# Experts placed among the shared expert's units in a mixture-of-experts layer, with sums that start from zero and are added by accumulating loads

## What is computed

```python
full_logits = x @ gate_w.T                       # 4096 tokens x (8 experts + 1 shared)
rw   = weights of up to 4 experts of each token  # sparse mixer, top-p 0.75, normalised
mask = (rw > 0) & (running count within the expert <= cap)   # cap = 640 tokens an expert
gw   = softmax(full_logits where allowed)
gd   = rw * sum(gw[:, :8])
out  = sum over experts e of gd[:, e] * down_e(silu(gate_e(x)) * up_e(x))   # 128 hidden units
out += gw[:, 8] * shared_down(silu(shared_gate(x)) * shared_up(x))          # 512 hidden units
x    = layernorm(x + out)
```

## Time and profile before

| | |
|---|---|
| median of 3 runs | 3832.75 us (3824.94 to 3836.05) |
| the profiled execution | 3839.45 us, span 3837.9 us |
| mean granted TensorE clock | 0.812 of full speed |
| the changed layer in the span | about 1584 to 1999.5 us |

### The profile page before, as it was taken

One profiled execution on the slowest core, in us unless ns is written; L12 is line 12 of the kernel. 1 busy time (PEld: TensorE's weight loads), 2 busy tenths in 40 slices (PEclk: granted clock), 3 DMA queues, 4 the chain that ended last, 5 costly groups with the idle time before them and its releaser, 6 DMA issues. The chain is left out here.

```text
span 3837.9 us, 34481 instructions
## 1 busy us (share of the span) xinstructions
PE 2848.2 (74%) x12664; PEld 1781.3 (46%) x12664; DVE 1739.6 (45%) x3573; ACT 1272.9 (33%) x1706; POOL 432.6 (11%) x405
## 2 busy tenths in 40 slices
PE   4667677585888888699816666666668888887887
PEld 2645445263333333454514444444446666664554
DVE  4535353543655666164225555555544445431222
ACT  3122131311554555322222222222246666561111
POOL 0110101010000000001541111111110111000000
PEclk9586777767899999799967777777788989997998
DMA  2000000003333332201350000000010100000000
GB/s 57 1 22 0 22 0 0 22 0 110 56 60 68 59 58 40 81 6 48 69 130 11 11 11 11 11 11 11 31 55 12 33 23 23 17 10 18 22 22 33
DMA packets 121228, 123.26 MB, mean 32 GB/s; under 512 B 38160, under 2 KB 108064, under 8 KB 121120
## 3 DMA queue, kind: packets, MB, share of 16 engines
q1 hardware_dynamic: 113440, 111.36, 11.2%
q0 software_dynamic: 7680, 10.49, 1.7%
HBM read 61.11 MB, written 35.26 MB: 25 GB/s over the span
## 5 line engine op out<-in xcount | busy, mean ns | idle before, releaser
L894 DVE TENSOR_REDUCE xattn_tops<-region 128x2 f32<-128x1024 f32 x256 | 305.7, 1220 | 144.4 <-PE region L700 144.3
L832 ACT ACTIVATE xattn_probs<-region 128x1024 f32<-128x1024 f32 x256 | 256.1, 1022 | 154.5 <-PE region L689 153.7
L1923 PE MATMUL region<-psi_fT 128*128 128x512 f32 x512 | 244.8, 622 | 21.9 <-DVE psi_low L2157 21.2
L122 PE MATMUL region<-gla_xT,weights_even 128*128 128x512 f32 (+1 forms) x416 | 197.9, 632 | 0.0
L689 PE MATMUL region<-xattn_qs,xattn_ks 49*128 49x512 f32 x512 | 125.5, 492 | 85.6 <-DVE xattn_tops L894 54.7
L114 PE MATMUL region<-ident,gla_xn 128*128 128x128 f32 x192 | 47.2, 427 | 186.9 <-DVE gla_xn L178 167.1
L114 PE MATMUL region<-ident,mamba_normed 128*128 128x128 f32 x64 | 15.7, 428 | 210.3 <-DVE mamba_normed L176 210.3
L1923 PEld LDWEIGHTS region<-psi_fT 128*128 128x128 f32 x512 | 97.2, 200 | 124.9 <-issue 100.5
L1944 PE MATMUL region<-psi_ctxv,psi_pT 128*128 128x65 f32 x1024 | 138.8, 301 | 20.3 <-issue 19.4
L1944 PEld LDWEIGHTS region<-psi_ctxv,psi_pT 128*128 128x128 f32 x1024 | 137.8, 219 | 29.3 <-issue 29.2
L122 PE MATMUL region<-mamba_xT,weights_odd 128*128 128x512 f32 x320 | 150.4, 632 | 0.0
(11 more groups left out here) (473 smaller groups left out, 5809.5 us busy)
## 6 DMA issues: line engine op xcount, KB each, us to landing
xattn_qs<-xattn_qhi SPq DMA_DIRECT2D x128, 64.0 KB, 2.3
xattn_ks<-xattn_khi SPq DMA_DIRECT2D x128, 64.0 KB, 2.3
gla_x<-in_x SPq DMA_DIRECT2D x8, 512.0 KB, 4.0
x_after_gla<-gla_x SPq DMA_DIRECT2D x8, 512.0 KB, 2.9
xattn_ctxT<-in_ctxT SPq DMA_DIRECT2D x8, 512.0 KB, 3.9
xattn_x<-x_after_gla SPq DMA_DIRECT2D x8, 512.0 KB, 4.1
xattn_qs<-xattn_qlo SPq DMA_DIRECT2D x64, 64.0 KB, 2.4
xattn_ks<-xattn_klo SPq DMA_DIRECT2D x64, 64.0 KB, 2.3
```

The source lines that it names most:

```text
L122: last = st.nc.tensor.matmul(o[0:m, i, :], w[:, c, col + i * P:col + i * P + m], rhs[:, c, :], start=c == 0, stop=c == kc - 1)
L832: A_(probs[:, p % 3, a, :, :], st.region(f"k{v}")[:], ACT.Exp).then_inc(st.emptying(f"k{v}"), 1)
L894: V.tensor_reduce(tops[:, n % 2, t, a::2], st.region(f"q{u}")[:], AX, ALU.max).then_inc(st.emptying(f"q{u}"), 1)
L1923: last = mm(o[:, a, :], fT[:, h, 0, t * P:t * P + P], fT[:, h, 1 + a, :], start=True, stop=True)
```

## The change

Four things change, all in `moe_layer`.

1. The eight experts are spread among the shared units: `turned` gives the unit in which an expert's `turn_rows` and `hidden` stand (18, 19, 20, 21, 23, 24, 25, 26); `down` and `add` follow in the next unit. All five finds of an expert stand in one unit (15 to 22), with its gather at the end.
2. There are six places for gathered rows: three as before, and three in `xT`, where batches' transposed rows are no longer needed. The places in `xT` wait for `begin` of the batches that lay there.
3. `sums` starts from zero: SP writes zeros to all of it (ten DMAs) behind the loads of the layer's input, and stores no rows of `xs` in it. The preamble's clearing and its wait are gone.
4. `finish b`: POOL issues an accumulating load that adds 512 rows of `sums` to the batch's rows in `xs` on the chip. The eight of them wait until all adds have landed. They take the place of SP's eight plain loads.

In `hidden`, ScalarE now writes into the tile `he` itself, instead of `silu`, so that it does not share a buffer with the shared units.

```diff
-        NX, EG, SP_, XE = B * NT, 4, CAP // P, 3
+        NX, EG, SP_, XE = B * NT, 4, CAP // P, 6
...
-        xe = [st.sb(f"xe{i}", [SP_, D]) for i in range(XE)]
+        xe = [st.sb(f"xe{i}", [SP_, D])[:] for i in range(XE - 3)]
+        used = xT[:].rearrange("p b c n -> p (b c n)")
+        xe += [used[:, i * 1280:i * 1280 + 1280].rearrange("p (k d) -> p k d", k=SP_) for i in range(3)]
...
-                V.memset(ye[0], 0.0).then_inc(st.sem("zeroed"), 1)
+                V.memset(picked[:], 0.0)
...
-                sp.wait_ge(st.sem("zeroed"), 1)
-                sp.dma_start(sums[B * T:, :].rearrange("(k p) d -> p k d", p=P), ye[0]).then_inc(st.sem("cleared"), 16)
                 weights.arrive(sp)
-                sp.wait_ge(st.sem("cleared"), 16)
...
+            turned = {18: 0, 19: 1, 20: 2, 21: 3, 23: 4, 24: 5, 25: 6, 26: 7}
             for u in range(B * SHF):
                 b, f = divmod(u, SHF)
-                finds = found[5 * (u - 16) // 2:5 * (u - 15) // 2] if u >= 16 else []
+                finds = [(u - 15, k) for k in range(SP_)] if 15 <= u < 15 + NE else []
+                if u in turned:
+                    yield "turn_rows", turned[u], 0
                 yield "gate", b, f
-                for n, (e, k) in enumerate(finds):
-                    if n == 1:
-                        yield "up", b, f
+                for e, k in finds[0:2]:
                     yield "find", e, k
-                    if k == SP_ - 1:
-                        yield "gather", e, 0
-                if not finds:
-                    yield "up", b, f
+                yield "up", b, f
+                for e, k in finds[2:4]:
+                    yield "find", e, k
+                if u in turned:
+                    yield "hidden", turned[u], 0
                 if f == 1 and b:
                     yield "shared_down", b - 1, 0
+                if u - 1 in turned:
+                    yield "down", turned[u - 1], 0
+                    yield "add", turned[u - 1], 0
+                for e, k in finds[4:]:
+                    yield "find", e, k
+                    yield "gather", e, 0
...
             yield "shared_down", B - 1, 0
-            yield "turn_rows", 0, 0
+            for b in range(B - 1):
+                yield "finish", b, 0
+            yield "measure", 0, 0
             yield "begin", B - 1, 0
-            for e in range(NE):
-                yield "hidden", e, 0
-                if e + 1 < NE:
-                    yield "turn_rows", e + 1, 0
-                yield "down", e, 0
-                yield "add", e, 0
-            for b in range(B + 1):
+            yield "finish", B - 1, 0
+            for b in range(1, B + 1):
...
-                for b in range(B):
-                    sp.wait_ge(st.sem("begun"), b + 1)
-                    sp.dma_start(sums[b * T:b * T + T, :].rearrange("(t p) d -> p t d", p=P), xs[:, b, :, :]).then_inc(
-                        st.sem("sums_out"), 16)
-                sp.wait_ge(st.sem("sums_out"), 16 * B)
-                sp.wait_ge(st.sem("added"), 16 * SP_ * NE)
-                for b in range(B):
-                    sp.dma_start(xs[:, b, :, :], sums[b * T:b * T + T, :].rearrange("(t p) d -> p t d", p=P)).then_inc(
-                        st.sem(f"x_in{b}"), 16)
+                zeros = picked[:].rearrange("p a n -> p (a n)")
+                for n in range((B * T + CAP) // T + 1):
+                    part = sums[n * T:min(n * T + T, B * T + CAP), :].rearrange("(t p) d -> p t d", p=P)
+                    sp.dma_start(part, times(zeros, part.shape[1])).then_inc(st.sem("zeroed"), 16)
...
+                    elif what == "finish":
+                        pool.wait_ge(st.sem("added"), 16 * SP_ * NE)
+                        pool.wait_ge(st.sem("begun"), b + 1)
+                        G.dma_start(xs[:, b, :, :], sums[b * T:b * T + T, :].rearrange("(t p) d -> p t d", p=P),
+                                    accum_op=ALU.add).then_inc(st.sem(f"finished{b}"), 16)
```

More of the change, by code:

```diff
@@ L986, in moe_layer @@
         source, target = st.sb("source", [NE, SP_], U32), st.sb("target", [NE, SP_], U32)
-        picked, ranks = st.sb("picked", [2, P]), f3(expert[:, 0:2 * P], 2)
+        picked, ranks = st.sb("picked", [2, P]), f3(expert[:, 6400:6400 + 2 * P], 2)
         shift = st.sb("shift", [2, NT])
@@ L1033, in order @@
             yield "logits", B - 1, 0
-            found = [(e, k) for e in range(NE) for k in range(SP_)]
+            turned = {18: 0, 19: 1, 20: 2, 21: 3, 23: 4, 24: 5, 25: 6, 26: 7}
             for u in range(B * SHF):
                 b, f = divmod(u, SHF)
-                finds = found[5 * (u - 16) // 2:5 * (u - 15) // 2] if u >= 16 else []
+                finds = [(u - 15, k) for k in range(SP_)] if 15 <= u < 15 + NE else []
+                if u in turned:
+                    yield "turn_rows", turned[u], 0
                 yield "gate", b, f
-                for n, (e, k) in enumerate(finds):
-                    if n == 1:
-                        yield "up", b, f
+                for e, k in finds[0:2]:
                     yield "find", e, k
-                    if k == SP_ - 1:
-                        yield "gather", e, 0
-                if not finds:
-                    yield "up", b, f
+                yield "up", b, f
[3 more added lines that the diff above has]
+                    yield "hidden", turned[u], 0
                 if f == 1 and b:
                     yield "shared_down", b - 1, 0
+                if u - 1 in turned:
[4 more added lines that the diff above has]
+                    yield "gather", e, 0
                 if u < 8:
@@ L1231, in _ @@
                         act.wait_ge(*st.full(f"xe{b}"))
-                        if b == 0:
-                            act.wait_ge(*st.emptied(f"find{NE - 1}_{SP_ - 1}"))
                         if b >= 2:
@@ L1241, in _ @@
                         act.wait_ge(*st.full(f"gue{b}"))
-                        act.wait_ge(*st.emptied(f"gue{b - 1}" if b else f"gu{B - 1}_{SHF - 2}"))
-                        A_(silu[:, 0, :], st.region(f"gue{b}")[:, 0, :], ACT.Silu).then_inc(st.sem("silu"), 1)
+                        if b >= 2:
+                            act.wait_ge(*st.full(f"ye_end{b - 2}"))
+                        A_(he[b % 2][:, 0:T], st.region(f"gue{b}")[:, 0, :], ACT.Silu).then_inc(st.sem("silu_e"), 1)
                         act.wait_ge(*st.full(f"gue_end{b}"))
-                        act.wait_ge(*st.emptied(f"gue_end{b - 1}" if b else f"gu{B - 1}_{SHF - 1}"))
-                        A_(silu[:, 1, 0:P], st.region(f"gue_end{b}")[:, 0:P], ACT.Silu).then_inc(st.sem("silu"), 1)
+                        A_(he[b % 2][:, T:CAP], st.region(f"gue_end{b}")[:, 0:P], ACT.Silu).then_inc(st.sem("silu_e"), 1)
             @block.vector
@@ L1394, in _ @@
                         n = SP_ * b + i
+                        if n == 0:
+                            dve.wait_ge(st.sem("zeroed"), 16 * 10)
                         dve.wait_ge(st.sem("ranked"), n + 1)
@@ L1408, in _ @@
                     elif what == "hidden":
-                        n = SHF * B + 2 * b
-                        dve.wait_ge(st.sem("silu"), n + 1)
-                        if b >= 2:
-                            dve.wait_ge(*st.full(f"ye_end{b - 2}"))
-                        TT(he[b % 2][:, 0:T], silu[:, 0, :], st.region(f"gue{b}")[:, 1, :], ALU.mult).then_inc(
+                        dve.wait_ge(st.sem("silu_e"), 2 * b + 1)
+                        TT(he[b % 2][:, 0:T], he[b % 2][:, 0:T], st.region(f"gue{b}")[:, 1, :], ALU.mult).then_inc(
                             st.emptying(f"gue{b}"), 1)
-                        dve.wait_ge(st.sem("silu"), n + 2)
-                        TT(he[b % 2][:, T:CAP], silu[:, 1, 0:P], st.region(f"gue_end{b}")[:, P:2 * P], ALU.mult).then_inc(
-                            st.emptying(f"gue_end{b}"), 1)
+                        dve.wait_ge(st.sem("silu_e"), 2 * b + 2)
+                        TT(he[b % 2][:, T:CAP], he[b % 2][:, T:CAP], st.region(f"gue_end{b}")[:, P:2 * P],
+                           ALU.mult).then_inc(st.emptying(f"gue_end{b}"), 1)
                     elif what == "down":
@@ L1450, in gather @@
                         pool.wait_ge(*st.full(f"xe_end{e - XE}"))
+                    elif e >= XE - 3:
+                        pool.wait_ge(st.sem("begun"), e - 1)
                     for k in range(SP_):
@@ L1456, in _ @@
                 for what, b, i in work:
-                    if what == "gather" and b < XE:
+                    if what == "gather":
                         gather(b)
-                    elif what == "turn_rows" and b + XE < NE:
-                        gather(b + XE)
                     elif what == "add":
+                        pool.wait_ge(st.sem("targets"), b + 1)
                         if b == 0:
-                            pool.wait_ge(st.sem("targets"), NE)
-                            pool.wait_ge(st.sem("sums_out"), 16 * B)
```

(1 more changed line is left out.)

7 lines of the change are left out of this document (3 added, 4 removed).

## The result

The changed kernel takes 3776.87 us (median of 4 runs, 3765.88 to 3782.18) against 3830.84 us for the kernel before on the same chip: a ratio of 0.9856, 95% interval 0.9829 to 0.9883. The profiled execution took 3782.18 us.

The account below looks back on a forecast made before the run. TensorE bounds the shared units, then POOL's queue sets the end; the next block at 1950.2 instead of 1999.55 us saves 49.3 us, taken from the 3832.75 us median: 3783.4 us, 8-in-10 range 3765 to 3806.

Parts of the forecast that it names:

- the signs that I had named for being wrong: Adds ending behind TensorE's work, load issues longer than the landings' spacing, or a granted clock falling in the units.
- The front: Layer start: without the clearing's wait ahead of the input loads, TensorE starts 5 us earlier, bounds 3 and 6.6.
- The experts move into TensorE's stage and cost all of it there: Shared units: the experts' 60.6 us of TensorE work cost fully there; the adds land by 1899.7 us, TensorE ends at 1908.1.
- the stall rival: Merged stage: `down` on VectorE waits for late adds and holds up TensorE; 12 us go back, 3795 us; chance 0.10.
- The correction of 3.5 us at units 15 to 17: TensorE: a new wait for `steps` of 1 to 2.5 us plus waits for banks add 3.5 us, bounds 2 and 7.
- my count back: Expert and POOL times reckoned backwards from TensorE's end at 1908.1 us, placing the last add's issue at 1895.9 us.
- The accumulating loads' pace: Layer end: at the adds' 146 ns a packet, the DMA engines take 4.67 us a batch; likeliest case, chance 0.45.
- POOL's issue: Issue cost of one accumulating load on POOL: bounds 1.25 and 7.4 us, 5.2 us at 4.7 ns a descriptor.
- the rival in which it sets the pace: POOL's issue of 5.2 us a load paces the layer's end: 35.4 us less, 3797.4 us; chance 0.27.
- 65.5 us: Rival at the layer's end: loads run at nearly the plain rate, saving 65.5 us, 3767.2 us; chance 0.13.
- The tail behind the eighth norm: Layer end: from the start of the eighth norm to the next block takes 10.4 us, as in the kernel before.

Follow-up runs that it names:

- the front alone: The kernel before with only the spare rows' clearing moved behind the input loads and its preamble wait removed: 3826.36 us, ratio 0.9985.
- the changed kernel again: The changed kernel without any edit, measured once more on another experiment's chip: 3777.20 us, ratio 0.9850 to the kernel before.
- the stores-wait profile: The changed kernel with SP's output stores held until all eight accumulating loads have landed: 3771.94 us, ratio 0.9852 to the kernel before.
- the plain load: The changed kernel with POOL's loads not accumulating, so input and shared expert's part are missing from the output: 3771.86 us, ratio 0.9852 to the kernel before.
- the kernel with vector adds: The changed kernel with SP loading `sums` into `xT` and VectorE adding it, replacing the accumulating loads: 3784.72 us, ratio 0.9890 to the kernel before.
- finds in twos: The changed kernel with at most two finds between other products, the first two behind unit 15's `up`: 3776.09 us, ratio 0.9844 to the kernel before.

## Why the prediction was right

The forecast was 49.3 us less by one likely way, and 54 us (3830.84 - 3776.87) were measured. That the spreading carries the saving was right and is shown. That the number came so close is in part luck, because two terms were off in opposite directions: the last add was issued 7.0 us later than I had it (1902.87 against 1895.9 us), and the tail behind it was 10.9 us shorter (43.4 against 54.3). The next block came at 1946.25 us and not at 1950.2. With the first error alone the saving would have been 42 us, with the second alone 60. One of the signs that I had named for being wrong did appear: the granted clock fell in units 15 to 17.

- **The front**, 5 us with bounds 3 and 6.6: TensorE's first transpose came 5.3 us earlier with the front alone and in the changed kernel, and 3.9 us in the changed kernel again, the least of all profiles. Right, and shown by the front alone.
- **The experts move into TensorE's stage and cost all of it there; POOL's adds end before TensorE.** Right: without the spreading the ratio is 0.9986 and not 0.9856. TensorE was busy 20.00 of 20.00 us in the mixed units, at full clock, and ended at 1914.98 us, 8.0 us behind the last landing (and 6.9 us later than my 1908.1). `down` on VectorE never waited for adds, so the stall rival did not occur.
- **The correction of 3.5 us at units 15 to 17**, bounds 2 and 7. The two waits stood where I had put them, 0.74 and 0.52 us. But the stretch from `steps` to expert 0's rows took 42.0 us in the profile after, where my sum has about 36, and 32.8 to 44.3 us over six profiles with the same order: the same products with nearly the same waits differ by 11.5 us with the clock, more than my bounds of 2 and 7 us allow. Because `steps` itself came 3.1 us earlier than I had it (1712.6 us), expert 0's rows were only 2.9 us late. The other 4.1 us of the 7.0 lie between them and the last add: 148.3 us, where my count back has 144.2.
- **The accumulating loads' pace, 4.67 us a batch.** This term was mis-sized: they land 2.65 us apart when nothing else runs. The step that failed is to take the adds' share of engine time, 146 ns a packet, as the pace of the loads. It failed twice. Most of it is that a packet of these loads is not a packet of the adds: by the same division it takes 101 ns, not 146. The rest is that packets overlap on an engine (123.1% in the stores-wait profile), so that 32 of them take 2.65 us, 83 ns each. What I had left out is that the stores share the engines; beside them the last loads land 4.1 to 4.4 us apart. From the first norm's start to the eighth's, 1913.29 to 1935.78 us, it is 3.2 us a load, against 4.67.
- **POOL's issue**, between 1.25 and 7.4 us, estimated at 5.2 us for the rival in which it sets the pace. It is 1.35 us, near the lower bound. If the 0.53 us against the plain load were all for a second read of each row, that would be 1.0 ns a row, not 4.7; the plain load also has a quarter of the packets, so it is at most that. That rival is refuted. The trace agrees with the Trainium skill's statement ("DMA: Bandwidth & Descriptors", "Anatomy of one DMA") that descriptor generation is small. An estimate by its fit for the bytes moved, 1.2 us a batch, does not hold for an accumulating load, which takes 2.65.
- **Where the loads' part ended.** The engines set the pace of the loads, as I had it: the eighth was issued at 1918.28 us, right behind the last `begin`, and landed 17.5 us later behind the others. But their pace alone, 2.65 us, is nearer to the plain rate's 1.53 than to my 4.67. The measured saving lies between the two, 49.3 and 65.5 us.
- **The tail behind the eighth norm**, 10.4 us: 10.5 us.

Two parts of the change bring nothing that these runs can tell: the six places, and the accumulating loads together with the zero start by themselves. What the zero start does is to allow the spreading at all. That follows from the program and not from a run: the adds need no stored rows of `xs`, so that they can begin at unit 19, while before POOL waited ahead of the first add until all eight batches were stored, and so for the eighth batch's `begin`. The accumulating loads are not needed for it, since the kernel with vector adds is spread too.

Open stays why the granted clock stood at half in most of 1716 to 1748 us. It stood there behind a wait of 0.74 us and around one of 0.52 us, and with finds in twos, without these waits, it stayed at full; other differences between the two orders were not tried apart. An earlier fall, around 1704 to 1712 us behind a wait of 2.19 us in the routing, stands with either order. And nearly the same waits went with unlike clocks: in windows of 8 us from 132 us behind the issue on, it was down to 0.50 in three of the six profiles and no lower than 0.79 in the three others.

## What to carry to other kernels

Where one engine is the bound in one stage and a DMA chain in the next, moving the second stage's products into the first costs their full time there, and pays all the same if the chain then runs beside them (this layer went from 416.4 us to 362.7 in one profile and 372.7 in another). Ask which dependency kept the chain from beginning, not which engine is busy.

Read a rate from a spacing of landings or from bytes in a saturated window, not from a share of busy time divided by packets: the packets overlap, and those of another kind of transfer take another time.

The cost of a stretch on TensorE may lie in its clock and not in its waits (here 1.3 us of waits). The clock also differs between executions: two profiles of one kernel are 10.1 us apart in this layer. Compare stretches that the clock does not touch, or many runs.

## What the hardware showed that I had not expected

An accumulating load from DRAM onto the chip runs at 2.65 us for 512 KB, some 198 GB/s, and costs POOL 1.35 us of issue for 512 rows; the plain one costs 0.82 us, in a quarter of the packets. The granted clock in the first 30 us of TensorE's work in the layer was 0.61 in some executions and 0.50 in others of the same instructions, and moved the end of the routing from 129.0 to 135.5 us and more (136.8).
